# Causal attention: zeroing the exponentials of later keys on GpSimd, in place of a mask under the shifted scores

## What is computed

```python
q = layernorm(x)      # (16, 128, 256) -> heads (16, 16, 128, 16)
k = v = ctx
scores = einsum('bhqd,bhkd->bhqk', q, k) * 16 ** -0.5
scores = where(k_index > q_index, -inf, scores)      # causal
m = scores.max(-1)
x = x + tanh(g_xattn[3]) * softmax(scores) @ v
```

## Time and profile before

| | us |
|---|---|
| median of 3 runs | 2379.8 |
| lowest and highest | 2371.12, 2379.82 |
| the profiled execution | 2377.23 |
| its span in the trace | 2375.4 |
| start of the stage (first transfer and memset) | 2121.26 |
| first exponential of the stage | 2153.78 |
| first instruction of the next stage | 2272.04 |

### The profile page before, as it was taken

The page is one execution under the profiler, slowest core; times in us unless marked ns, Lnnn a source line. Parts: engine busy times, 40 slices in busy tenths (PEclk is TensorE's granted clock), DMA queues, the critical chain, the costliest instruction groups (busy, mean ns, idle before and its releaser), DMA issues. The chain is left out here.

```text
span 2375.4 us, 49288 instructions
## 1 busy us (share of the span) xinstructions
PE 2047.6 (86%) x17593; PEld 1100.0 (46%) x17617; DVE 1697.0 (71%) x3048; ACT 1339.2 (56%) x1808; POOL 873.4 (37%) x730
## 2 busy tenths in 40 slices
PE   3776999999997785899996789999999999558855
PEld 1343555556564564488863423333333333434533
DVE  4775755555555557843356899999999999567975
ACT  3454633333335675633332568888888888445565
POOL 4750000000002561500053347777777777224301
PEclk8887999999997897999996755555555555788989
DMA  6343222222224007222322036666666665010110
GB/s 206 89 173 120 71 65 68 62 71 66 66 66 142 24 2 268 84 50 68 64 80 98 1 58 107 108 107 107 107 108 107 108 108 108 13 71 2 20 21 27
DMA packets 384870, 195.32 MB, mean 82 GB/s; under 512 B 312301, under 2 KB 355311, under 8 KB 382703
## 3 DMA queue, kind: packets, MB, share of 16 engines
q1 hardware_dynamic: 381617, 184.47, 32.5%
q0 software_dynamic: 3072, 8.39, 1.1%
HBM read 94.99 MB, written 23.09 MB: 50 GB/s over the span
## 5 line engine op out<-in xcount | busy, mean ns | idle before, releaser
L2429 POOL CAST qa_pT<-qa_eT 128x2048 bf16<-128x2048 uint8 x256 | 483.4, 1893 | 162.1 <-DMA qa_eT<-qa_e 120.8
L2442 PE MATMUL qa_S<-qa_kT,qa_qT 32*128 32x512 f16 x1024 | 514.4, 616 | 4.8 <-DVE qa_scores L2494 3.4
L2478 ACT ACTIVATE qa_e<-qa_scores,qa_nb 128x2048 uint8<-128x2048 f32 x256 | 510.4, 1994 | 4.4
L2494 DVE TENSOR_SCALAR_CACHE_REDUCE qa_scores<-qa_S,qa_sq,qa_mx 128x1024 f32<-128x1024 f32 x256 | 335.8, 1358 | 0.0
L2494 DVE TENSOR_SCALAR_CACHE_REDUCE qa_scores<-qa_S,qa_sq 128x1024 f32<-128x1024 f32 x256 | 320.2, 1297 | 3.4 <-PE qa_S L2442 3.4
L2452 PEld LDWEIGHTS qa_O<-qa_V,qa_pT 128*128 128x128 bf16 x4096 | 128.4, 105 | 215.6 <-issue 201.5
L1116 POOL MEMSET rms_nothing<- 128x512 f16 x1 | 0.5, 524 | 580.3 <-POOLq L3474 580.3
L973 PE MATMUL moe_G<-hT,moe_W 128*128 (+1 forms) x792 | 193.7, 381 | 7.1 <-DVE moe_zero L941 7.1
L982 PE MATMUL moe_O<-moe_W,moe_ap 128*128 (+1 forms) x1584 | 194.6, 273 | 4.3 <-DVE moe_ap L937 4.3
L913 ACT ACTIVATE moe_ap<-moe_a 128x512 f16<-128x512 f32 x132 | 83.1, 629 | 195.8 <-DVE moe_a L935 195.8
L973 PE MATMUL moe_U<-hT,moe_W 128*128 (+1 forms) x792 | 192.7, 379 | 0.0
(11 more groups left out here) (438 smaller groups left out, 3408.3 us busy)
## 6 DMA issues: line engine op xcount, KB each, us to landing
moe_wb<-weights_T SPq DMA_DIRECT2D x264, 128.0 KB, 2.9
moe_W<-in_moe_w SPq DMA_DIRECT2D x40, 384.0 KB, 11.9
moe_W<-in_moe_w SPq DMA_DIRECT2D x11, 1152.0 KB, 16.9
moe_xs_rows<-rms_nothing SPq DMA_DIRECT2D x46, 128.0 KB, 1.9
moe_ys_rows<-moe_ys SPq DMA_DIRECT2D x23, 256.0 KB, 2.1
conv_rows<-conv_parts SPq DMA_DIRECT2D x16, 256.0 KB, 2.9
qa_eT<-qa_e SPq DMA_TRANSPOSE x256, 3.1
conv_qst<-conv_rows SPq DMA_DIRECT2D x96, 32.0 KB
```

What stands on the lines that cost most here:

```text
L2429: nc.gpsimd.tensor_copy(pT[:, u % RING, :, :].rearrange("p (b r) q -> p b r q", r=2), pairs).then_inc(s_cast, 1)
L2442: last = nc.tensor.matmul(S[:, n % SLOTS, q * QW:(q + 1) * QW], qT[rows, g, t * P:(t + 1) * P], kT[rows, g, first:first + QW], start=True, ...
L2478: nc.scalar.activation(e8[:, u % RING, :], scores[:, u % RING, :], ACT.Exp, bias=nb[:, p % 2, i:i + 1], accum_out=sums[:, u:u + 1]).then_i ...
L2494: nc.vector.tensor_scalar(scores[:, u % RING, half * HW:(half + 1) * HW], S[:, n % SLOTS, :], sq[:, t, h:h + 1], mx[:, u % RING, 0:1] if h ...
```

## The change

The mask has one side only, the one for the scores. The shifted scores are written by their products alone, each of which now opens its own sum. The mask's second triangle, its memset and its select are gone. A new function on GpSimd, `later_keys_cut`, waits for the exponential of a half and sets the entries with a key behind the query to zero, in place; its semaphore `s_cut` is what the value products wait for. GpSimd's queue, which was a plain loop over the stacks, is written anew: the stacks of tiles 0 to 2, and then for each tile the cut of half 0, the stacks of tile t+3, the cut of half 1.

```diff
-        maskf = sb("maskf", [P, 2, HALF, P])
-        mask = sb("mask", [P, 2, HALF, P], BF16)
+        maskf = sb("maskf", [P, HALF, P])
+        mask = sb("mask", [P, HALF, P], BF16)
...
-                nc.gpsimd.memset(maskf[:, :, :, :], 0.0).then_inc(s_set, 1)
+                nc.gpsimd.memset(maskf[:, :, :], 0.0).then_inc(s_set, 1)
...
-                nc.gpsimd.affine_select(out=maskf[:, 1, :, :], in_=maskf[:, 1, :, :], compare_op=ALU.is_ge, fill=LOW,
-                                        base=0, pattern=[[0, HALF], [1, P]], channel_multiplier=-1).then_inc(s_mask, 1)
...
-                for t in range(NB):
+                def stacks(t):
...
+                def later_keys_cut(t, r):
+                    pool.wait_ge(s_E, 2 * t + r + 1)
+                    e = E[:, r, :, :, :].rearrange("p j i q -> p (j i) q")
+                    nc.gpsimd.affine_select(out=e, in_=e, compare_op=ALU.is_ge, fill=0.0,
+                                            base=0, pattern=[[0, NG], [1, P]], channel_multiplier=-1).then_inc(s_cut, 1)
+
+                for t in range(AHEAD):
+                    stacks(t)
+                for t in range(NB):
+                    later_keys_cut(t, 0)
+                    if t + AHEAD < NB:
+                        stacks(t + AHEAD)
+                    later_keys_cut(t, 1)
...
-                act.wait_ge(s_mask, 2)
+                act.wait_ge(s_mask, 1)
...
-                def masked(out, side, r, rows_used, left, right, done):
-                    for j in range(2):
-                        nc.tensor.matmul(out[:, j, :, :], sh.ident16[:, :], mask[:, side, :, :], start=True, stop=False, skip_group_check=True)
+                def products(out, r, rows_used, left, right, opens, done):
                     for i in range(HALF):
...
-                                                    start=False, stop=True, skip_group_check=True)
+                                                    start=opens, stop=True, skip_group_check=True)
...
-                    masked(ST, 1, r, PARTS + 1, kT[:, t % 4, :, :], qT2[:, t % 2, :, :], s_ST)
+                    products(ST, r, PARTS + 1, kT[:, t % 4, :, :], qT2[:, t % 2, :, :], True, s_ST)
...
-                    pe.wait_ge(s_E, 2 * t + r + 1)
+                    pe.wait_ge(s_cut, 2 * t + r + 1)
```

More of the change, by code:

```diff
@@ L2934, in causal_attention @@
         (s_set, s_mask, s_mask16, s_stats, s_mv, s_std, s_rstd, s_shift, s_norm, s_qhi, s_qlo, s_khi, s_klo, s_vx, s_TQ, s_TK, s_T2, s_qT, s_kT, s_q2,
-         s_S1, s_max, s_neg, s_ST, s_E, s_O, s_oT, s_B, s_inv, s_on, s_res) = map(sem, (
+         s_S1, s_max, s_neg, s_ST, s_E, s_cut, s_O, s_oT, s_B, s_inv, s_on, s_res) = map(sem, (
              "set", "mask", "mask16", "stats", "mv", "std", "rstd", "shift", "norm", "qhi", "qlo", "khi", "klo", "vx", "TQ", "TK", "T2", "qT", "kT",
-             "q2", "S1", "max", "neg", "ST", "E", "O", "oT", "B", "inv", "on", "res"))
+             "q2", "S1", "max", "neg", "ST", "E", "cut", "O", "oT", "B", "inv", "on", "res"))
         next_weights.prepare(ctx)
@@ L2958, in _ @@
                 pool.wait_ge(s_set, 4)
-                nc.gpsimd.affine_select(out=maskf[:, 0, :, :], in_=maskf[:, 0, :, :], compare_op=ALU.is_ge, fill=LOW,
+                nc.gpsimd.affine_select(out=maskf[:, :, :], in_=maskf[:, :, :], compare_op=ALU.is_ge, fill=LOW,
                                         base=0, pattern=[[0, HALF], [-1, P]], channel_multiplier=1).then_inc(s_mask, 1)
-                nc.gpsimd.affine_select(out=maskf[:, 1, :, :], in_=maskf[:, 1, :, :], compare_op=ALU.is_ge, fill=LOW,
-                                        base=0, pattern=[[0, HALF], [1, P]], channel_multiplier=-1).then_inc(s_mask, 1)
                 nc.gpsimd.memset(ks[:, :, :, PARTS:PARTS + 1], 1.0).then_inc(s_set, 1)
                 nc.gpsimd.memset(vx[:, :, :, HD:HD + 1], 1.0).then_inc(s_set, 1)
-                for t in range(NB):
+                def stacks(t):
                     q = sh.H[:, t, :].rearrange("p (h d) -> p h d", d=HD)
@@ L3023, in _ @@
                         normalise(2 * c + 1)
-                act.wait_ge(s_mask, 2)
-                nc.scalar.activation(mask[:, :, :, :], maskf[:, :, :, :], ACT.Copy).then_inc(s_mask16, 1)
+                act.wait_ge(s_mask, 1)
+                nc.scalar.activation(mask[:, :, :], maskf[:, :, :], ACT.Copy).then_inc(s_mask16, 1)
                 normalise(4)
@@ L3169, in scores @@
                         pe.wait_ge(s_max, 2 * t + r)
-                    masked(S1, 0, r, PARTS, qT[:, t % 2, :, :], kT[:, t % 4, :, :], s_S1)
+                    for j in range(2):
+                        nc.tensor.matmul(S1[:, j, :, :], sh.ident16[:, :], mask[:, :, :], start=True, stop=False, skip_group_check=True)
+                    products(S1, r, PARTS, qT[:, t % 2, :, :], kT[:, t % 4, :, :], False, s_S1)
                 def shifted_scores(t, r):
```

## The result

| | before | changed |
|---|---|---|
| median, us | 2378.95 (4 runs, one more than ahead of the prediction) | 2413.57 (4 runs) |
| lowest and highest | 2371.12 to 2379.82 | 2410.95 to 2417.21 |
| profiled execution, and its span | 2377.23, 2375.4 | 2417.21, 2415.5 |
| the stage, set-up memset to the next stage's | 150.8 (2121.26 to 2272.04) | 186.8 (2123.77 to 2310.56) |
| mean granted clock, whole program | 0.796 | 0.786 |

The ratio is 1.0154, 95% interval 1.0128 to 1.018: 35 us slower. Between the two profiled executions lie 40.0 us: 36.0 in the stage, 2.5 ahead of it, where nothing was changed, and 1.5 behind it.

The account below looks back on a forecast made before the run. VectorE was taken as the bound of the causal attention stage. From 2377.2 us, -1.4 + 17.3 + 1.4 + 1.5 + 5 = +23.8 gave 2401.0, and +11 for the clock 2412 us; 8 in 10 range 2394 to 2441.

Parts of the forecast that it names:

- What bounds: Causal attention stage: VectorE, busy 37.2 of 40 us, is fuller than TensorE; little of 17.3 us of mask products on the path.
- The ring: Stacks of t+3 wait behind tile t's first select, closing a loop through four engines: 8.94 against 7.61 us, +17.3 in 13 tiles.
- VectorE beside GpSimd: First selects and casts on GpSimd slow down beside VectorE's work on the next weights: +5 us, bounds 0 and 6.
- The clock: TensorE's pause ahead of the query transposes lowers its clock in half of 13 tiles, 1.65 us each: +11; chance 0.46.
- The ends: Last tiles: longer spacing from 13 to 15 and one uncovered select behind the last exponential pair, together +1.5 us.
- Prologue: Set-up on GpSimd loses one select and half a memset, -1.05; with -0.36 at the first exponential, together -1.4 us.
- first tile: Tile at the low clock: the new wait breaks TensorE's dense stretch before the rise to full clock, +1.4 us.
- ports: GpSimd and VectorE share a pair of ports, so both lose when working side by side: +5 us, bounds 0 and 6.

Follow-up runs that it names:

- run 4: Kernel before, without the mask products under the shifted scores and with nothing in their place; 2376.4 us, ratio 0.9982.
- Run 3: Kernel before with its masks and no select, only GpSimd's queue order taken from the changed kernel; 2400.9 us, ratio 1.0083.
- run 1: Changed kernel, all selects kept, but GpSimd makes the stacks one tile earlier (t+4 in place of t+3 between the cuts); 2382.4 us, ratio 1.0021.
- Run 5: Changed kernel with seven more identity-and-mask products per tile on TensorE ahead of the waiting query transposes; 2414.2 us beside 2391.4, ratio 1.0083.

## Why the prediction was right, step by step

- **What bounds: VectorE, not TensorE.** Held: removal alone is worth 2 to 4 us of 17.3 (run 4); the prediction had priced it at next to nothing.
- **The ring.** Held, and named as the decisive step. Run 3 has it without the select, +20 us (13 of them with the clock up); run 1 has the select without the ring, +4. The place is the one given, the transposes of the queries of t+3. Clean tiles take 8.64 us for 8.94. By the prediction's own steps 0.10 us is gained up to the transposes, where the select is 1.09 us for 1.17; 0.09 from there to the end of the second shifted scores, which without their mask start 0.24 us after the scores' products start and not 0.33; 0.06 in the second select; and 0.05 behind it. So 13 x 1.03 = 13.4 us for the 17.3 forecast. One step was taken as binding that hardly is: the prediction adds the second select in full, and TensorE's own work ends within 0.1 us of it in the clean tiles and after it in the others.
- **VectorE beside GpSimd.** +5 forecast with bounds 0 and 6. In the changed kernel the first selects of tiles 3 to 13 are 4.4 us longer than 1.09 in sum, the casts of the queries another 1.6 over 0.74: 6.0, the upper bound, of which 1.0 (tile 13) belongs to the ends. Run 5, with the clock up from tile 1 to 12, has a mean of 8.96 for a clean 8.64, which is 4.1 in 13 tiles. Only some pieces interfere strongly: the selects beside the whole-width ones took 2.12 us, the one beside two pieces of 1024 1.55, those beside four pieces of 256 1.16 to 1.25, and beside VectorE's wide sums (2.27 us) 1.09 as alone. "SBUF — State Buffer", section "Who interferes with whom", of the Trainium skill says that where GpSimd and a VectorE operation in a two-port mode meet, the one issued later is blocked for the whole of the other's instruction. The trace comes near it: VectorE's piece ran its 1.22 us from 2205.89, and the select that started 0.04 later took 1.03 more than alone, where 1.18 was left of the piece.
- **The clock.** The direction was right and the size too small. The mean spacing is 10.19 against 8.96 with the pause filled: 16.1 us. Of these 1.35 are tile 0 (10.07 for 8.72), which the prediction had as a term of its own, 1.4. The other 14.8, for the 11 forecast, come from nine tiles at 1.6 on average. The price of one, 1.65, was right, and the number, half of 13, too small. The nine are of two kinds: 2.3 us where the clock was down before the query transposes, 1.2 to 1.4 where it fell behind them. "TensorE: Matmul & The Clock Gate", section "HAM oscillation — how this bites in real kernels", of the Trainium skill tells of a loop in which a wait in every step throttles the array again in every step; by the prediction's reckoning that would have been +21. The waits of that loop are 3 to 5 us, and the longest here in tiles 1 to 12 was 2.65, so the page does not speak of pauses like these. The trace lies between the two numbers: nine of the twelve tiles, not all.
- **The ends.** Prologue and first exponential together: 31.14 us from the set-up memset for 32.52 before, -1.4 as forecast. Behind tile 13 the stage took 23.1 us for 19.3: +3.8 for the 1.5 forecast. Of this 2.3 are two selects that nothing covers (one each in tiles 14 and 15), and 1.5 is the clock, which the prediction had left out here: the value products of tile 15 took 1.08 us for 0.65 before, and the granted clock from 2301 us on was 0.50 for 1.00. Run 5 has 22.2, with the same slow products at the end.
- **The sum** came out by terms that err both ways: ring 13.4 for 17.3, first tile 1.35 for 1.4, clock 14.8 for 11, ports 4.1 (by run 5) for 5, ends with the prologue +2.4 for +0.1. In the stage 36.0 us for 34.8. That the median of 2413.6 lies 1.6 us from the forecast of 2412 is therefore in part luck: the ring is 3.9 too dear and the clock 3.8 too cheap.

One statement in the prediction did not hold as worded: "TensorE wait ... a smaller one of the second value products for the select". The list has 0.6 us for it, in three tiles, because the products before it end just then; in the ten others the select had ended before TensorE came.

## What to carry to other kernels

When work is added to an engine that has free time, look first at what stands behind it in that engine's queue and how far ahead the engine was running. Here the added selects cost about 6 us where that order was kept clear of them (run 1 beside run 4), and the removed products were worth 2 to 4; putting the stacks of a later tile behind a wait of the present one cost 20 us by itself, and moving them one tile forward in the same queue gave all but 3 to 4 us of 35 back. A second bill may come behind such a wait: a pause of 1 to 2 us in each tile that TensorE did not have before took its clock down in most tiles, and dull work in the pause was cheaper than the pause.

## What I had not expected of the hardware

- The clock fell behind pauses much shorter than the 3.16 us of the earlier trace rows: in run 3 behind 0.69 and 1.10 us with 1 us of work between in three tiles, and behind 1.39 in a fourth. In the kernel before, with pauses of 0.68 and up to 1.0 us in a tile of 7.6, it never did between 2160 and 2260 us.
- 91 extra products of 128x512 made the kernel 17 us faster by the ratios (12 by the medians).
- GpSimd's select over 128x1024 took 1.09 us beside 0.64 for 128x512, 0.45 for 512 elements more; the memset of the set-up, 0.53 us for 512 and 0.96 for 1024, has nearly the same step.
